# One transformer layer on one core: the first head group's row maxima move into the first stage, the late weights to the attention stage's end, and the attention planner picks by due times

## What is computed

```python
def reference(x, W_qkv, W_proj, w_gate, w_up, w_down):
    x = layernorm(x + attention(x, W_qkv, W_proj))   # softmax(q k^T / 4, causal) v, then W_proj
    wg, wu, wd = w_gate / 127, w_up / 127, w_down / 127
    return layernorm(x + (silu(x @ wg.T) * (x @ wu.T)) @ wd.T)
```

## Time and profile before

| | us |
|---|---|
| median of 3 runs (lowest, highest) | 1407.6 (1406.67, 1409.45) |
| the profiled execution | 1410.0 |
| its span | 1408.3 |
| first stage: first q matmul to last v matmul | 22.7 to 172.9 |
| first exponential of group 0 | 202.4 |
| first exponential of group 31 | 1014.0 |
| last matmul with v | 1048.2 |

### The profile page before, as it was taken

How to read it: one execution, slowest core, us unless ns; L and a number is a source line. 1 busy time by engine, 2 the same in 40 slices (tenths; PEclk the granted TensorE clock), 3 DMA queues, 4 the chain that set the end, 5 groups by cost and what they waited for, 6 DMA issues and landing times.

```text
span 1408.3 us, 29921 instructions
## 1 busy us (share of the span) xinstructions
PE 1319.4 (94%) x11732; PEld 639.7 (45%) x11732; DVE 1125.3 (80%) x1665; ACT 906.6 (64%) x2003; POOL 346.2 (25%) x448
## 2 busy tenths in 40 slices
PE   4999989999999999999999999999989999999997
PEld 3555533333333333333333333333335656656664
DVE  4776588988888888988988888888526887877876
ACT  2555437788788778778778788788764443443433
POOL 2000001122221221221221221222113443443534
PEclk9999959999999999999999999999889999999999
DMA  5777541123222121121121221220011212122111
GB/s 201 223 217 231 183 115 44 40 56 98 61 59 57 40 71 44 41 71 45 42 71 43 49 63 44 52 64 17 12 31 39 77 59 90 49 87 90 47 61 46
DMA packets 152317, 106.63 MB, mean 76 GB/s; under 512 B 79712, under 2 KB 139616, under 8 KB 152176
## 3 DMA queue, kind: packets, MB, share of 16 engines
q1 hardware_dynamic: 152176, 104.71, 26.2%
HBM read 62.13 MB, written 41.94 MB: 74 GB/s over the span
## 4 chain that ended last, share of the span: by engine, by line
PE 73%; DVE 12%; ACT 7%; issue 4%; SPq 1%; POOL 1%; DMA 1%; DVEq 0%; POOLq 0%; ACTq 0%
PE ps L1209 18%; PE ps L1194 12%; PE ps L1302 12%; DVE row_max L912 9%; PE ps L1168 6%; PE ps L1317 5%; ACT probs L729 4%; PE ps L1112 4%; PE ps L1249 4%; PE ps L1221 3%; PE ps L1131 3%; PE ps L1173 3%; PE ps L1287 1%; PE ps L1241 1%; ACT x_hi_rows L759 1%
## 5 line engine op out<-in xcount | busy, mean ns | idle before, releaser
L729 ACT ACTIVATE probs<-ps 128x512 f32<-128x512 f32 (+3 forms) x1536 | 641.4, 503 | 174.0 <-PE ps L1194 172.6
L912 DVE TENSOR_REDUCE row_max<-ps 128x2 f32<-128x1024 f32 (+1 forms) x512 | 569.2, 1153 | 41.8 <-PE ps L1173 19.9
L1194 PE MATMUL ps<-q_stack,k_stack 50*128 50x512 f16 (+3 forms) x1536 | 375.9, 332 | 19.8 <-ACT probs L729 13.4
L1209 PE MATMUL ps<-probs,v_ones 128*32 128x512 f32 (+3 forms) x3072 | 330.4, 502 | 4.1 <-POOL probs L620 2.7
L620 POOL TENSOR_SCALAR_AFFINE_SELECT probs<-probs 128x512 f32<-128x512 f32 x256 | 163.2, 637 | 676.1 <-ACT probs L729 674.4
L1168 PE MATMUL ps<-k_stack,q_stack 48*128 48x512 f16 (+3 forms) x1536 | 290.8, 334 | 9.3 <-DVE row_max L912 4.5
L1194 PEld LDWEIGHTS ps<-q_stack,k_stack 50*128 50x128 f16 x1536 | 109.1, 93 | 289.5 <-ACT probs L729 230.5
L642 POOL TENSOR_TENSOR h_lo<-h_sb,h_hi 128x512 f16<-128x512 f32 x96 | 119.4, 1250 | 196.9 <-ACT h_hi L778 196.9
L1173 PE MATMUL ps<-above,one_of_half 64*128 64x128 bf16 (+1 forms) x2048 | 154.4, 205 | 0.0
L770 ACT ACTIVATE silu<-ps 128x512 f32<-128x512 f32 x96 | 57.4, 597 | 135.5 <-PE ps L1302 135.5
L1173 PEld LDWEIGHTS ps<-above,one_of_half 64*128 64x128 bf16 x2048 | 127.2, 96 | 34.9 <-issue 2.4
(11 more groups left out here) (129 smaller groups left out, 1461.8 us busy)
## 6 DMA issues: line engine op xcount, KB each, us to landing
x_sb<-in_L_attn_x SPq DMA_DIRECT2D x32, 512.0 KB, 5.2
qk_parts<-parts SPq DMA_DIRECT2D x64, 256.0 KB, 2.5
q_stack<-qk_parts SPq DMA_DIRECT2D x192, 64.0 KB, 2.3
k_stack<-qk_parts SPq DMA_DIRECT2D x192, 64.0 KB, 2.3
v_rows<-v_sb SPq DMA_DIRECT2D x16, 512.0 KB, 3.2
v_flat<-v_rows SPq DMA_DIRECT2D x32, 256.0 KB, 3.1
attn_rows<-attn_sb SPq DMA_DIRECT2D x64, 128.0 KB, 2.1
v_sb<-attn_rows SPq DMA_DIRECT2D x16, 512.0 KB, 6.1
```

The source lines that it names most:

```text
L729: act.activation(probs[(NS * n + s) % RING][:, j, 0:w], ps[:, 4 + use % 3, 0:w], ACT.Exp, scale=scale_of_batch).then_inc(exp_done, 1)
L912: dve.tensor_reduce(row_max[:, half, :, p, qt], banks[:, :, 0:w], AX.X, ALU.max).then_inc(s_free, 1)
L1194: pe.matmul(ps[:, 4 + use % 3, 0:w * P], k_stack[n % NG][rows, p, tile_cols(kt)], q_stack[n % NG][rows, p, q0:q0 + w * P], start=True, sto ...
L1209: last = pe.matmul(ps[32 * j:32 * j + 32, 7, c0:c0 + w * P], v_ones[n % 2][:, kt, j, :], probs[(NS * n + s) % RING][:, j, 0:w * P], start= ...
```

## The change

- **Planner.** Each possible step gets a due time. "st" is due when it could start or 1000 ns before ACT's planned work runs out, whichever is later; "max" the same with DVE, and more when maxima are over 1.5 groups ahead; "pv" 600 ns from now, or 2400 ns ago when the ring of probabilities is full; "mT", "oT" and the new "wt" 500 ns before they could start. A step that could start only later than now is charged twice the wait. The smallest sum is taken.
- **First maxima.** The 20 units of group 0 run in chunks 4 to 13 of the first stage, two per chunk, through bank pair 2 and 3 alone (`FIRST_MAXIMA`, `pair_of`); PE computes one behind the q outputs and one behind the k outputs, DVE reduces one behind `part_lo(c, 1)` and one at the chunk's end. The six outputs of a chunk now rotate over four banks, 4 to 7 (`qkv_bank`, `wait_for_bank`).
- **Loads.** SP issues the unit rows and the stacks of group 0 behind chunk 2, those of groups 1 and 2 with v behind chunks 4 and 6, and those of group 3 behind chunk 8.
- **x and v.** x is split two chunks ahead, behind the k parts and the scales, and ACT copies both v outputs.
- **POOL.** The casts of the MLP's integer weights and the presets come before the shared maxima of batches 1 to 7.
- **Late weights.** They become 13 steps "wt", possible once all maxima are planned and before the turned output of group 30's second half; they use the bank pairs, and DVE copies them.

The diff, cut to its core (the moved functions `row_maxima`, `split_max` and `scores_for_max` differ only in the bank pair and, for group 0, in one wait):

```diff
-def attention_order(groups, slots, diagonal, units):
+def attention_order(groups, slots, diagonal, units, weights):
...
-    ROWS_MOVED = 2700
-    LEAD_ST, LAG_MAX, GROUPS_AHEAD = 0.2, 1.5, 2
+    ROWS_MOVED, WEIGHT = 2700, (350, 450)
+    KEEP_ACT, KEEP_DVE, KEEP_PV, KEEP_TURN, FULL, WHOLE = 1000, 1000, 600, 500, 3000, 20000
+    LAG_MAX, GROUPS_AHEAD = 1.5, 2
     ns, nu, hg = len(slots), len(units), 4
+    mx = nu
...
-    banks = pairs = st = mx = pv = turned = 0
-    rows, parts, ready, pv_end = {}, {}, {}, {}
+    banks = pairs = st = pv = turned = turned_w = 0
+    rows, parts, ready, pv_end = {}, {0: 0}, {}, {}
...
         could = []
         if turned in parts:
-            could.append((max(bank[banks % 3], parts[turned]), -9, "mT"))
-        if turns:
-            could.append((max(turns[0][2], pair[pairs % 2]), -8, "oT"))
+            could.append((max(bank[banks % 3], parts[turned]), "mT"))
+        if mx == groups * nu and turned_w < weights:
+            could.append((pair[pairs % 2], "wt"))
+        if turns and (turns[0][:2] != (groups - 2, 1) or turned_w == weights):
+            could.append((max(turns[0][2], pair[pairs % 2]), "oT"))
         if mx < groups * nu and mx // nu <= pv // ns + GROUPS_AHEAD:
-            could.append((pair[pairs % 2], mx / nu - LAG_MAX, "max"))
+            could.append((pair[pairs % 2], "max"))
         if st < groups * ns * hg and st // hg < pv + RING and st // hg // ns in rows:
-            could.append((max(bank[banks % 3], rows[st // hg // ns]), st / (ns * hg) - LEAD_ST, "st"))
+            could.append((max(bank[banks % 3], rows[st // hg // ns]), "st"))
         if pv in ready:
-            could.append((max(ready[pv], o_free if slots[pv % ns][1] == 0 else 0), pv / ns, "pv"))
-        now = [c for c in could if c[0] <= pe + 20] or [min(could)]
-        start, _, what = min(now, key=lambda c: c[1])
+            could.append((max(ready[pv], o_free if slots[pv % ns][1] == 0 else 0), "pv"))
+        best = None
+        for avail, kind in could:
+            if kind == "st":
+                due = max(avail, act - KEEP_ACT)
+            elif kind == "max":
+                due = max(avail, dve - KEEP_DVE) + max(0, mx / nu - pv / ns - LAG_MAX) * WHOLE
+            elif kind == "pv":
+                due = max(avail, pe) + (KEEP_PV if st // hg < pv + RING else KEEP_PV - FULL)
+            else:
+                due = avail - KEEP_TURN
+            late = due + 2 * (max(pe, avail) - pe)
+            if best is None or late < best[0]:
+                best = (late, max(pe, avail), kind)
+        _, start, what = best
         pe = max(pe, start)
...
+        elif what == "wt":
+            pe += WEIGHT[0]
+            dve = max(dve, pe + PE_DVE) + WEIGHT[1]
+            pair[pairs % 2] = dve + MAX_END + DVE_PE
+            order.append(("wt", turned_w))
+            turned_w, pairs = turned_w + 1, pairs + 1
...
-        pair_use = {step: n for n, step in enumerate(s for s in order if s[0] in ("max", "oT"))}
-        PAIR_USES = GROUPS * (NU + 2)
+        pair_use = {("max", 0, u): u for u in range(NU)}
+        pair_use.update({step: NU + n for n, step in enumerate(s for s in order if s[0] in ("max", "oT", "wt"))})
+        PAIR_USES = GROUPS * (NU + 2) + len(late_units)
+        FIRST_MAXIMA = {4 + k: (2 * k, 2 * k + 1) for k in range(NU // 2)}
+
+        def pair_of(use):
+            return 1 if use < NU else use % 2
+
+        def qkv_bank(c, n):
+            return 4 + (6 * c + n) % 4
+
...
-            for c in range(NCH - 2):
-                chunk_a(c)
-
...
-            for m in range(4):
-                sp.wait_ge(parts_stored[m], 16 * (T // CH + 1))
-            sp.wait_ge(w_cast, 3)
-            sp.wait_ge(preset, 4)
-            for g in range(4):
-                for i in range(2):
-                    row = i * SIDE + ROWS
-                    sp.dma_start(k_stack[g][row:row + 2, :, :], unit_rows[:]).then_inc(unit_rows_loaded, 16)
-            for par in range(2):
-                load_stacks(0, range(par, len(PAIRS), 2))
-                chunk_a(NCH - 2 + par)
-            for m in range(4):
-                sp.wait_ge(parts_stored[m], 16 * (NCH + 1))
-            for par in range(2):
-                sp.wait_ge(v_stored[par], 16 * (NCH // 2 + 1))
-            load_v(0)
-            load_stacks(1)
-            load_v(1)
-            load_stacks(2)
-            load_stacks(3)
+            for c in range(NCH):
+                chunk_a(c)
+                if c == 2:
+                    for m in range(4):
+                        sp.wait_ge(parts_stored[m], 16 * (T // CH + 1))
+                    for par in range(2):
+                        sp.wait_ge(v_stored[par], 16 + 16)
+                    sp.wait_ge(w_cast, 3)
+                    sp.wait_ge(preset, 4)
+                    for g in range(4):
+                        for i in range(2):
+                            row = i * SIDE + ROWS
+                            sp.dma_start(k_stack[g][row:row + 2, :, :], unit_rows[:]).then_inc(unit_rows_loaded, 16)
+                    load_stacks(0)
+                elif c in (4, 6):
+                    load_v(c // 2 - 2)
+                    load_stacks(c // 2 - 1)
+                elif c == 8:
+                    load_stacks(3)
 
...
+                    if step[1] == 0:
+                        for m in range(4):
+                            sp.wait_ge(parts_stored[m], 16 * (NCH + 1))
+                        for par in range(2):
+                            sp.wait_ge(v_stored[par], 16 * (NCH // 2 + 1))
...
                 pool.wait_ge(w_loaded[name], 16)
                 pool.tensor_copy(b_[:], n_[:]).then_inc(w_cast, 1)
                 pool.wait_ge(w_cast, k + 1)
...
+                share_x_max(b)
 
...
                 act.wait_ge(parts_stored[m], 16 * c + 16)
-                act.copy(parts[m][:, HI, :], ps[:, 2 + m, :]).then_inc(part_hi_done, 1)
+                act.copy(parts[m][:, HI, :], ps[:, qkv_bank(c, m), :]).then_inc(part_hi_done, 1)
 
             def chunk_a(c):
-                if c + 1 < NCH:
-                    split_x_hi(c + 1)
                 part_hi(c, 0)
                 part_hi(c, 1)
                 if c + 1 < NCH:
                     copy_xt_hi(c + 1)
                 part_hi(c, 2)
                 part_hi(c, 3)
-                act.wait_ge(v_ready, 2 * c + 4 + 1)
+                if c + 2 < NCH:
+                    split_x_hi(c + 2)
                 act.wait_ge(v_stored[c % 2], 16 * (c // 2) + 16)
-                act.copy(v_sb[c % 2][:, 0:2, :].rearrange("p t d -> p (t d)"), ps[:, 6, :]).then_inc(v_copied[0], 1)
+                for k in range(2):
+                    act.wait_ge(v_ready, 2 * c + 4 + k + 1)
+                    act.copy(v_sb[c % 2][:, 2 * k:2 * k + 2, :].rearrange("p t d -> p (t d)"),
+                             ps[:, qkv_bank(c, 4 + k), :]).then_inc(v_copied[k], 1)
 
             split_x_hi(0)
             for u in EARLY_ORDER[0:2]:
...
                 chunk_a(c)
...
 
-            for u, unit in enumerate(late_units):
-                act.wait_ge(late_wt_ready, u + 1)
...
             def chunk_a(c):
-                if c + 1 < NCH:
-                    split_x_lo(c + 1)
                 part_lo(c, 0)
                 part_lo(c, 1)
+                if c in FIRST_MAXIMA:
+                    row_maxima(("max", 0, FIRST_MAXIMA[c][0]))
                 if c + 1 < NCH:
                     copy_xt_lo(c + 1)
                 if c + 3 < NCH:
                     x_maximum(c + 3)
                 part_lo(c, 2)
                 part_lo(c, 3)
-                dve.wait_ge(v_ready, 2 * c + 4 + 2)
-                dve.wait_ge(v_stored[c % 2], 16 * (c // 2) + 16)
-                dve.tensor_copy(v_sb[c % 2][:, 2:4, :].rearrange("p t d -> p (t d)"),
-                                ps[:, 7, :]).then_inc(v_copied[1], 1)
                 if c % 2 == 0 and c + 2 < NCH:
                     scales(c // 2 + 1)
+                if c + 2 < NCH:
+                    split_x_lo(c + 2)
+                if c in FIRST_MAXIMA:
+                    row_maxima(("max", 0, FIRST_MAXIMA[c][1]))
+                    if FIRST_MAXIMA[c][1] == NU - 1:
+                        split_max(0)
...
+            split_x_lo(1)
...
+                elif step[0] == "wt":
+                    use = pair_use[step]
+                    dve.wait_ge(s_ready, use + 1)
+                    dve.tensor_copy(late_units[step[1]][2],
+                                    unit_bank(late_units[step[1]], 2 * (use % 2))).then_inc(s_free, 1)
...
+            def wait_for_bank(c, n):
+                c0, n0 = divmod(6 * c + n - 4, 6)
+                if c0 >= 0 and n0 < 4:
+                    pe.wait_ge(qk_bank_free, 4 + 4 * c0 + n0 + 1)
+                elif c0 >= 0:
+                    pe.wait_ge(v_copied[n0 - 4], 1 + c0 + 1)
+
...
-                pe.wait_ge(qk_bank_free, 4 * c + m + 1)
+                wait_for_bank(c, m)
...
```

(74 more changed lines are left out.)

85 lines of the change are left out of this document (40 added, 45 removed).

## The result

The changed kernel takes 1391.0 us (median of 4 runs, 1390.27 to 1393.3); the kernel before took 1408.5 beside it (1406.67 to 1409.72). The ratio is 0.988, with an interval of 0.9864 to 0.9895: faster, by 17.5 us where 41 were forecast. 1391 lies inside the range, but it is the figure of rival 1, not of the forecast.

What follows compares the result with a forecast made beforehand. PE bounds the first stage; in the attention DVE is nearest its limit, waiting for PE's order. Start -19.3, planner -24.8, weights +3 give -41.1: profiled 1410.0 becomes 1368.9, median 1367 us, range 1336 to 1402 without rival 3 and the lowest twentieth.

Steps and rivals of the forecast that it cites:

- rival 1: Attention groups: the planner changes nothing, only the start and the weights count; 1391 us, chance 0.20.
- The front: Before the first chunk: POOL's casts beside DVE's preparation delay it by 0 to 3 us, taken as 1.
- Chunks without maxima: First stage, chunks 0 to 3, 14 and 15: they go at PE's pace, 6 x 8.69 = 52.1 us.
- Last v matmul to first exponential: Gap between first stage and attention: the 29.5 us become 6.
- Rival 4: Start of attention: PE's clock holds its low level for 23 us again, PE loses up to 11.5; 1378 us, chance 0.06.
- Pairs with maxima: First stage, chunks 4 to 13: DVE's late last reduction makes PE wait 0.8; a pair takes 19.4 us, five take 97.
- The later loads (6 us each) end before ACT needs the buffers again.: First stage, SP's queue: load batches after the first cost nothing; only 3 us, between 0 and 6, was charged.
- I take a gain of 0.8, about a third: 31 attention groups: the planner wins 0.8 of DVE's 2.7 us a group of waits for PE, 24.8 us.
- rival 2: Attention groups: DVE is kept nearly full, 1.7 of the 2.7 us a group go; 1339 us, chance 0.18.
- late weights, +3: Last group: 13 weight-turn units on PE cost 3 us, between -5 (PE's clock stays up) and +6.

Runs made afterwards that it cites:

- the spread version: Changed kernel with SP issuing the first stage's stacks, unit rows and v a few at a time between a chunk's own stores: 1377.8 us, ratio 0.9788.
- the new order of DVE: Changed kernel with loads issued between stores, and DVE taking a chunk's second maximum before it splits x: 1376.7 us, ratio 0.9769.
- halved engines: Changed kernel, half the columns cut: maxima 1392.5 us, exponentials 1365.2, products with v 1351.5, exponentials and maxima 1340.4, products and maxima 1349.1.
- The two half-changes: Kernel before with only the planner's due-time rule: 1398.6 us, ratio 0.993; changed kernel with the planner's old rule: 1405.0 us, ratio 0.9973.
- the later rows: Changed kernel with the planner's time for the max rows' way (`ROWS_MOVED`) at 4200 instead of 2700 ns: 1395.2 us, ratio 0.9908.

## Why the prediction was wrong

**Right.** *The front*: 0.9 us later, forecast 1 (the other runs with this front began at 23.5 to 24.7 us). The cause is seen too. In order of time, POOL and then DVE of the changed kernel:

```profile
14.23 1.46 POOL L620 CAST wgate_b<-wgate_n 128x1536 bf16<-128x1536 int32 x1
...
18.18 1.47 POOL L620 CAST wdown_b<-wdown_n 128x1536 bf16<-128x1536 int32 x1 [0.42 <-DMA wdown_n<-in_L_ffn_w_down]
```

```profile
14.50 1.21 DVE L873 SCALAR_TENSOR_TENSOR x_bound<-x_max_all 128x1 f32<-128x1 f32 x1
...
18.96 1.75 DVE L848 SCALAR_TENSOR_TENSOR x_lo_rows<-x_sb,x_scale,x_hi_rows 128x1024 f16<-128x1024 f32 x1 [2.56 <-ACT x_hi_rows L699]
```

The first instruction of the scales takes 1.21 us beside a cast, where the earlier trace rows have 0.15 without one, and the first split 1.75 where the same one took 1.28 before. *Chunks without maxima*: 8.69, to the digit. *Last v matmul to first exponential*: 5.4, forecast 6. *Rival 4*, the clock: it did not happen where it was looked for; the granted clock was 1.00 in the gap and 0.99 over the groups. It fell in chunk 4, where no rival had it. The rival also misread its row: 0.61 in the earlier trace rows is POOL's busy time, the clock beside it is 0.58, so that some 25 of the 29.5 us stood at the low level and not 23.

**Right in size, wrong in reason.** *Pairs with maxima*: 19.4 forecast, 19.5 behind the loads, 98.2 for the ten chunks of the spread version where 97 were forecast. The prediction let DVE's end of the second reduction set this. In the spread version PE waited for DVE's reductions next to nothing from 60 to 165 us, and it is busy for 99% of the stage; the new order of DVE, which moved that end, left the pair within 0.6 us:

```profile
PE ps L1200 <- DVE row_max L927: 0.6, 2, 0.3
```

So the pair is PE's own. 19.2, the shortest, less 17.38 leaves 1.8 for four units, some 0.46 each; the prediction's 0.3 was too small, and its wait for DVE made up for it: the right size was luck.

**Wrong, first step: "The later loads (6 us each) end before ACT needs the buffers again."** The prediction saw the wait of ACT for a store once, took 3 us for it together with PE's wait for the k stack, and then let the second, third and fourth batch of loads pass free. All three held ACT, and the stage became 13.4 us longer than forecast. Chunks 6 to 11, behind these three, took 66.0 us where 58.2 were forecast: 7.8. Chunks 4 and 5, behind the first batch, took 27.3 where 19.4 and the 3 were forecast: 4.9, of which 2.6 are the low clock behind PE's wait. The other 0.7 lie elsewhere in the stage. The second batch took SP 7.2 us (80.2 to 87.4) instead of 6; but what was left out is the store that stands behind it, with ACT behind the store, and that it lands only 4.9 us after its issue. The first stage ended 17.5 us later than before, where the prediction's bound was 14. The Trainium skill (DMA: Bandwidth & Descriptors, "Queues, rings and completion order") says that each DMA engine takes the descriptors of one queue in the order in which they were put there; the stores directly behind a load of x and twelve stack loads landed in 4.8 to 5.0 us, against a median of 2.5 in the kernel before, which agrees. But the landing alone did not hold ACT. In the kernel before, two stores behind a load of x alone (66.1 and 67.4 us) took 4.7 in the median and no such wait came of it, and in the spread version the median of all is still 3.6 and ACT waits for none of them: it is their late issue. Spreading the issues gave 15.4 us of the stage back, which settles this step.

**Wrong, second step: "I take a gain of 0.8, about a third".** The rule gave 0.22 us a group between the two profiles (0.26 and 0.33 with one part changed at a time). The share was read off DVE's waits, as if each wait that ended in PE were idle time of the kernel. But the earlier trace rows show PE itself at 782.6 of 811.6 us, 96%, in the same stretch, more than DVE's 87%; the prediction names DVE and ACT there and passes over PE, and rival 2's argument, "PE's work of a group fits well inside DVE's", contradicts that row. Where DVE waited, PE was mostly at work for somebody else, or stood in the coupling with ACT. The halved engines show that DVE's waits were no time to be won: 91 us less work on DVE bought nothing. What an order could still win is, by the halved engines, at most about the distance from 25.6 to 24.0, not DVE's 2.7. How much of that 1.6 an order with three score banks can reach was not tried. The rule did do what the earlier trace rows asked for, the turned output's wait, and that was worth a quarter of what was forecast.

**Wrong in sign: late weights, +3.** The last group came out 4.1 us shorter. The turns lie at 993 to 1001 us, almost all in front of the last group, and took three tiles in 0.34 us where the earlier trace rows have 0.50:

```profile
995.28 0.34 PE L1124 MATMUL ps<-ident_bf,wgate_b 128*128 128x128 bf16 x3
```

The tail's granted clock is 1.00 instead of 0.86. The two half-changes divide it: 31.1 us at 1.00 with the weights moved and the old rule, 32.7 at 0.90 with the rule alone (the last group of each):

```profile
1008.70:1039.80 31.10, 25.97 (x191) 9.62 (x189) 6.80 (x20) 21.60 (x51) 6.70 (x10) 1.00 0.04 10
```

```profile
1003.80:1036.50 32.70, 28.52 (x190) 10.74 (x187) 6.81 (x20) 21.50 (x51) 6.30 (x10) 0.90 0.04 9
```

So about 3 of the 4 come with the weights and the rest of the change, 1.5 with the rule alone. These are single profiles: with the later rows, and with the new order of DVE, the last group took 31.6 to 31.7 us at 0.95, so 2.5 to 4 us is what the runs bear out. Why the clock stayed up was not tried by itself; in the 10 us in front of the last group PE was busy for 8.4 us before and for all 10 now. The prediction had this as its lower bound of -5, from the 0.86 of the earlier trace rows, and put the value at the wrong end.

So rival 1's number came true by another way: the groups gained something, the tail gained, and SP's queue took back 13 us that no rival had.

## What to carry to other kernels

Before the waits of a busy engine are counted as time to be won, look in the same row at the engine that it waits for: here that one was at 96%, and most of the waits were not to be had. The busy share alone does not settle it, since relieving ACT shortened the groups with PE's list as it was. When a batch of loads is put into a queue that also stores what a producer overwrites, charge each batch with its issue time and the store's landing behind it, not the first batch alone; or issue the loads a few at a time between the stores, which was worth 13 us here. Taking half the work off one engine, then off two, is a cheap way to see who sets a coupled pace: here relieving DVE was worth nothing, relieving ACT 0.85 us, and both together 1.55.

## What the runs showed of the hardware

- DVE's 128x1 instruction beside a POOL cast took 1.21 us in place of 0.15, and a 128x1024 one 1.75 in place of 1.28 to 1.30; the two engines shared no data there. Both times that the 128x1 instruction was slow it ended within 0.02 us of the cast (15.71 and 15.69 us here, both at 35.64 in the earlier trace rows).
- The max rows' four small DMAs (4 KB each, 1.7 us in the median) landed only after up to 3.45 us in some groups. PE waited for them 12 times in the run, 8.2 us in all, and groups of 25.6 became 26.1 to 27.0 where it waited longest. Allowing for it in the order cost as much in all groups as it saved in these.
- Behind 3.6 us in which PE stood for the k stack, the granted clock was 0.61 from 65 to 70 us and 0.70 from 70 to 75, and a q product of 128x512 took 0.63 us in place of 0.38; with the loads spread, PE waited 0.5 us there and the clock was 1.00 over the whole stage.
